# A vision tokenizer kernel on one core: the product steps of a group placed one step later in TensorE's list

## The chip, the core and the metric

The kernel runs on one core of a Trainium2 chip. A core has a matrix engine (TensorE, PE in the profile, with its weight loads listed apart as PEld), a vector engine (VectorE, DVE), a scalar engine (ScalarE, ACT), GpSimd (POOL), SyncE (SP), which here only starts transfers, and DMA queues. Each engine works through its own list of instructions in order; a list waits for another only at a semaphore. The metric is the time of one execution on the device in microseconds (us). Of three runs of the kernel before, the median is 921.68 us (920.68 to 923.33).

## The reference, cut to what matters

```python
def tokens(x, gamma, beta, W, b):            # x: (64, 2, 104, 104)
    lu, ru, ld, rd = _shifts(x)              # the image moved by 4 pixels in four directions
    concat = jnp.concatenate((x, lu, ru, ld, rd), axis=1)
    mean = jnp.mean(concat, axis=(1, 2, 3), keepdims=True)
    var = jnp.var(concat, axis=(1, 2, 3), keepdims=True)
    normed = (concat - mean) * jax.lax.rsqrt(var + EPS)
    normed = normed * gamma[None] + beta[None]
    y = conv(normed, W, window_strides=(8, 8))   # 13 x 13 patches, 128 outputs each
    return (y + b).reshape(B, E, -1).transpose(0, 2, 1)
h = tokens(x, ...)
h = jnp.concatenate([cls_tok, h], axis=1)        # 170 tokens for each image
h = h + attention(_layernorm(h), ...)            # gated linear attention
h = h + experts(_layernorm(h), ...)              # 8 experts, 2 for each token
```

The change concerns the first stage, `tokens`, and the layer-norm statistics of its result.

## The kernel before

The program has three stages one after the other: tokens (to about 197 us), attention with routing (to about 540 us), experts and the final sums (to the end). Only the first is touched.

**Tiling.** The 64 images are worked on in 8 groups of 8, a group as 4 pairs of images; a pair has 340 tokens, which are 3 tiles of 128. For group g, in this order: SyncE loads the images (`load_group`), ScalarE sums and squares (`stats_squares`), VectorE copies and sums the edges (`stats_sums`, L1022 on), TensorE adds over the rows of an image (`stats`, L701 on), VectorE makes mean and variance (`stats_small`), ScalarE the reciprocal deviation (`rstd`), VectorE the shift (`shifts`), ScalarE the normalised image (`normalise`) and VectorE its edges (`normalise_edges`). Then TensorE turns patches into columns in 8 **fills** of PSUM (`transpose_fill`, L669 on, matmul line L680; fills 0 to 3 have 4, 3, 3, 3 transposes, fills 4 to 7 have 4, 4, 3, 3), and VectorE multiplies each fill by gamma into the arena (`scale_fill`, line L1066). When all eight are scaled, TensorE makes the group's tokens in 6 **product blocks** (`y_tiles`, line L697), each 10 matmuls, that is two tiles of five matmuls (the trace counts each of these matmuls twice). A pair is complete halfway in blocks 1 and 4 and at the end of blocks 2 and 5. VectorE adds the bias to a complete pair and stores it in h (`tokens_out`, L1088) and later takes its layer-norm statistics (`ln1_stats`, lines L1094 and L1098). After the last pair ScalarE and VectorE turn the statistics into factors (L1639, L1640), and the attention stage begins.

**What sets the order.** The lists are written by hand. In both engines `group(g, ...)` walks through steps k = 0 to 7: TensorE transposes fill k of group g and does a product block of group g - 1; VectorE scales fill k of group g and does the tokens and statistics of groups g - 1 and g - 2 and the image statistics of group g + 1. `group` is called for g = 0 to 8; for g = 8 there is nothing left to transpose (`tr=False`), for g = 0 there are no products (`y=False`), and for g = 7 and 8 no image statistics (`stat=False`). Below, F0 to F7 are the transposes of the fills and Y0 to Y5 the product blocks in TensorE's list.

**The waits that matter here:**

- Y0 of a group waits until VectorE has scaled all its fills (`tr_free`, first line of `y_tiles`).
- The fill of step k may be transposed when the fill four before it has been scaled (`tr_free`): four PSUM banks are used in turn.
- The four small matmuls of `stats(g + 1)`, at k = 3 after the fill, wait for `dsum_done`, which VectorE's `stats_sums(g + 1)` gives, and for `asum_done`, which ScalarE gives after squaring the edges that `stats_sums` has copied (L1478).
- `tokens_out` waits for its pair (`y_full`); the products of a pair wait for a free one of three banks (`h_added`).

Of the kernel before, what the change touches and what calls it, by code (L numbers as in the profile page):

```python
# [28 lines left out]
GPAIRS = GROUP // 2  # L29
PT = 2 * TOK  # L30
PTILES = -(-PT // 128)
# [80 lines left out]
def need(eng, sem, value):  # L112

    if not isinstance(value, int) or value > 0:
        eng.wait_ge(sem, value)
# [44 lines left out]
def build(nc, a, out_rows):  # L160
# [6 lines left out]
    with ExitStack() as ctx:  # L167
# [454 lines left out]
        def _(pe):  # L622
# [39 lines left out]
            def beta_turn():  # L662
                pe.wait_ge(S["bt_copied"], 2)
                for t in range(PTILES):
                    ins = pe.transpose(ps[5][:, 128 * t:128 * t + 128], bt_t[:, 128 * t:128 * t + 128], ident)
                ins.then_inc(S["bt_turned"], 1)
# [4 lines left out]
            def transpose_fill(g, par, k):  # L671
                if k == 0:
                    pe.wait_ge(S["xmn_done"], g + 1)
                if k == 4:
                    pe.wait_ge(S["xhn_done"], g + 1)
                    pe.wait_ge(S["xen_done"], g + 1)

                need(pe, S["tr_free"], 8 * g + k - 3)
                for n, (src, rows) in enumerate(fills[par][k]):
                    ins = pe.transpose(ps[k % 4][:, rows * n:rows * n + rows],  # L680
                                       src.rearrange("r a b -> r (a b)"), ident[0:rows, 0:rows])
                ins.then_inc(S["tr_full"], 1)

            def y_tiles(g, par, k):

                if k == 0:
                    pe.wait_ge(S["tr_free"], 8 * g + 8)
                for j in range(2 * k, 2 * k + 2):
                    pair, t = j // PTILES, j % PTILES
                    q = GPAIRS * g + pair  # L690
                    if t == 0:
                        need(pe, S["h_added"], q - len(TOKEN_BANKS) + 1)
                        if q == 1:
                            pe.wait_ge(S["bt_ready"], 1)
                    at = PT * pair + 128 * t
                    for s in range(NSHIFT):
                        ins = pe.matmul(ps[TOKEN_BANKS[q % len(TOKEN_BANKS)]][:, 128 * t:128 * t + 128],  # L697
                                        gx_all[par][:, s, at:at + 128], wt[:, s, :], start=s == 0, stop=s == NSHIFT - 1)
                    if t == PTILES - 1:
                        ins.then_inc(S["y_full"], 1)  # L700

            def stats(g):
                pe.wait_ge(S["dsum_done"], g + 1)
                pe.wait_ge(S["asum_done"], g + 1)
                need(pe, S["var_done"], g)
                x0 = cols["stat_all"][0]
                x1 = cols["stat_edge"][0]
                for k in range(2):
                    o = ps[6][0:HROWS, 2 * k:2 * k + 2]
                    pe.matmul(o, cst[0:HROWS, x0 + k * HROWS:x0 + (k + 1) * HROWS], st[0:HROWS, 0:2], start=True, stop=False)  # L710
                    ins = pe.matmul(o, cst[0:HROWS, x1 + k * HROWS:x1 + (k + 1) * HROWS], st[0:HROWS, 2:4],
                                    start=False, stop=True)
                ins.then_inc(S["stat_ps"], 1)

            def group(g, par, tr=True, y=True, stat=True):
                for k in range(8):
                    if tr:
                        transpose_fill(g, par, k)
                    if (g, k) == (1, 0):
                        beta_turn()  # L720
                    if k == 3 and stat:
                        stats(g + 1)
                    if 1 <= k <= GPAIRS * PTILES // 2 and y:
                        y_tiles(g - 1, 1 - par, k - 1)

            patch_transposes(0, "gam_flat", "gam_ps")
            stats(0)
# [242 lines left out]
        def _(dve):  # L970
# [23 lines left out]
            def beta_out():  # L994
                dve.wait_ge(S["cleared"], CLEAR_BET)
                dve.wait_ge(S["bet_ps"], 1)
                patches_out(1, "bet_ready")
# [24 lines left out]
            def stats_sums(g, par, u):  # L1022
                dve.wait_ge(x_loaded[par], 16 * GROUP_DMAS * (u + 1))

                need(dve, S["xen_done"], g)
                need(dve, S["asum_done"], g)
                need(dve, S["stat_ps"], g)
                x3 = xh[par][0:HROWS, :].rearrange("r (cp w) -> r cp w", w=SIDE)
                ch.link(dve.tensor_copy(xe[0:HROWS, 0, :, HALF:PATCH], x3[:, :, 0:HALF]))
                dve.tensor_copy(xe[0:HROWS, 1, :, 0:HALF], x3[:, :, SIDE - HALF:SIDE]).then_inc(S["edge_done"], 1)  # L1030
                dve.wait_ge(S["edge_done"], g + 1)
                dve.tensor_reduce(st[0:HROWS, 2:3], xe[0:HROWS].rearrange("r a b c -> r (a b c)"), AX_X, ALU.add)\
                   .then_inc(S["dsum_done"], 1)

            def stats_small(g):
                dve.wait_ge(S["stat_ps"], g + 1)
                m = st[0:HROWS, 4:8].rearrange("r (k a) -> r k a", k=2)
                ch.link(dve.tensor_scalar(st[0:HROWS, 4:8], ps[6][0:HROWS, 0:4], 1.0 / N_CONCAT, None, ALU.mult))
                ch.link(dve.tensor_tensor(st[0:HROWS, 8:10], m[:, :, 0], m[:, :, 0], ALU.mult))
                dve.tensor_tensor(st[0:HROWS, 10:12], m[:, :, 1], st[0:HROWS, 8:10], ALU.subtract).then_inc(S["var_done"], 1)  # L1040
# [42 lines left out]
            def tokens_out(g, k):  # L1083

                dve.wait_ge(S["y_full"], GPAIRS * g + k + 1)
                src = ps[TOKEN_BANKS[(GPAIRS * g + k) % len(TOKEN_BANKS)]][:, 0:PCOLS].rearrange("p (t n) -> p t n", t=PTILES)
                hp = h[:, bass.ds(GPAIRS * g + k, 1), :, :].rearrange("p o t n -> p (o t) n")
                dve.tensor_tensor(hp, src, bt[:, :, :], ALU.add).then_inc(S["h_added"], 1)  # L1088

            def ln1_stats(g, k):  # L1090
                dve.wait_ge(S["h_added"], GPAIRS * g + k + 1)
                need(dve, S["ln1_stats"], GPAIRS * g + k - 1)
                for t in range(PTILES):
                    ch.step(dve.bn_stats(bns1[:, k % 2, t], h[:, bass.ds(GPAIRS * g + k, 1), t, :].rearrange("p o n -> p (o n)")))  # L1094
                ch.settle()
                for t in range(PTILES):
                    tile = bass.ds(PTILES * GPAIRS * g + PTILES * k + t, 1)
                    ins = dve.bn_aggr(mv1[:, tile, :].rearrange("p o m -> p (o m)"), bns1[:, k % 2, t])  # L1098
                    if t < PTILES - 1:
                        ch.step(ins)  # L1100
                ins.then_inc(S["ln1_stats"], 1)

            def group(g, par, base, u, tr=True, y=True, stat=True):
                ch.start(base)
                for k in range(8):
                    if k == 1 and stat:
                        stats_sums(g + 1, 1 - par, u)
                    if k == 4 and stat:
                        stats_small(g + 1)
                    if k in (3, 4, 6, 7) and y:  # L1110
                        tokens_out(g - 1, (3, 4, 6, 7).index(k))
                    if k == 5 and stat:
                        shifts(g + 1)
                    if tr:
                        scale_fill(g, par, k)
                    if (g, k) == (0, 2):
                        beta_out()
                    if (g, k) == (0, 4):
                        weights_out()
                    if (g, k) == (0, 7):  # L1120
                        beta_products_out()
                    if (g, k) == (1, 0):
                        beta_tokens_out()
                    if k in (0, 1) and g >= 2:
                        ln1_stats(g - 2, k + 2)
                    if k in (5, 7) and y:
                        ln1_stats(g - 1, (5, 7).index(k))
                    if k == 6 and stat:
                        normalise_edges(g + 1, 1 - par)
                if not tr:  # L1130
                    for k in range(2, GPAIRS):
                        ln1_stats(g - 1, k)
                return ch.n
# [16 lines left out]
            for g in range(1, NGROUP - 1):  # L1150
                dbase += group(g, g % 2, dbase, (g + 1) // 2)
# [563 lines left out]
```

## Time and profile before

| | |
|---|---|
| median of 3 runs | 921.68 us (920.68 to 923.33) |
| profiled execution | 921.47 us, span from first to last instruction 919.7 us |
| busy: PE, PEld | 801.1 us (87%), 684.4 us (74%) |
| busy: DVE, ACT, POOL | 743.3 us (81%), 571.0 us (62%), 504.0 us (55%) |
| mean granted TensorE clock | 0.943 of full speed |
| chain that ended last, shares of the whole | PE 47%, DVE 28%, issue 10% |
| the product blocks, L697 | 960 matmuls in the trace, 123.9 us busy, idle before them 12.0 us, ended by DVE's L1066 |
| scaling of fills, L1066 | 160 instructions, 71.8 us busy, idle before them 12.7 us, ended by PE's L680 |

The profile is of one execution, so sums are made against its 921.47 us. "Idle before" is time in which the engine did nothing, and the releaser is what it had been waiting for. A granted clock of 1.00 is 2.4 GHz, 0.50 is 1.2 GHz. Matmuls overlap each other, so the time that the trace gives for a row of them reaches a little beyond the start of the next row; the distance between two starts is the better measure.

### The profile page before, as it was taken

The page shows a single profiled execution, that of the slowest core. Times are in us where ns is not written, and L with a number is a line of the kernel's source. Part 1 is how long each engine was busy: PE and PEld are TensorE (multiplying, and loading weights), DVE is VectorE, ACT ScalarE, POOL GpSimd, SP SyncE. Part 2 cuts the span into 40 slices and gives each one's busy share as a digit, 9 for nine tenths or more (in the row PEclk, how much of TensorE's full clock was granted, in tenths as well). Part 3 has the DMA queues.
Part 4 walks back from the last instruction along what each step waited for, and adds up shares of the span by engine and source line. Part 5 has one row for each costly group of instructions (what it writes and reads, how often), then busy time and mean ns, then how long its engine had stood idle before and what let it go on. Part 6 is the DMA issues. An engine that isn't in the chain of part 4 may idle for free.

```text
span 919.7 us, 27974 instructions
## 1 busy us (share of the span) xinstructions
PE 801.1 (87%) x7821; PEld 684.4 (74%) x7822; DVE 743.3 (81%) x3194; ACT 571.0 (62%) x1536; POOL 504.0 (55%) x660
## 2 busy tenths in 40 slices
PE   1799999888999999999999638999999999999910
PEld 1699999875677777777777526999999999999910
DVE  2768777833789999989999752999999999999987
ACT  2633344015889999999999523666676666676610
POOL 3000000000078888888788782778877777877850
PEclk9999999998999999999999558999999999999965
DMA  8544330034011212122121226422222222222489
GB/s 181 124 80 82 61 62 1 1 115 144 23 55 54 60 57 62 54 60 60 51 63 55 63 86 206 164 80 76 79 73 76 74 74 73 80 74 76 125 299 376
DMA packets 68637, 84.19 MB, mean 92 GB/s; under 512 B 12118, under 2 KB 52745, under 8 KB 68157
## 3 DMA queue, kind: packets, MB, share of 16 engines
q1 hardware_dynamic: 52727, 53.27, 21.4%
q0 software_dynamic: 12256, 22.50, 7.9%
q10 hardware_dynamic: 3555, 7.23, 2.3%
q8 instruction: 49, 0.80, 0.4%
q14 instruction: 50, 0.39, 0.2%
HBM read 48.15 MB, written 35.71 MB: 91 GB/s over the span
## 4 chain that ended last, share of the span: by engine, by line
PE 47%; DVE 28%; issue 10%; ACT 4%; DMA 3%; SPq 2%; DVEq 2%; ACTq 1%; POOL 1%; POOLq 0%
PE ps L697 9%; DVE arena L1400 7%; PE ps L797 5%; DVE arena L1066 4%; PE ps L772 4%; DVE arena L1421 3%; PE ps L783 3%; PE ps L846 3%; PE ps L832 3%; PE ps L851 3%; PE ps L778 2%; DVE arena L1383 2%; PE ps L865 2%; PE ps L956 2%; PE ps L761 2%
## 5 line engine op out<-in xcount | busy, mean ns | idle before, releaser
L578 POOL DMA_INDIRECT x_slots<-arena x192 | 191.9, 1000 | 58.1 <-POOL arena L576 45.7
L607 POOL DMA_INDIRECT y_tokens<-arena x184 | 187.4, 1018 | 46.1 <-issue 45.2
L956 PE MATMUL ps<-arena 128*128 x1472 | 180.5, 276 | 0.2 <-ACT arena L1663 0.2
L956 PEld LDWEIGHTS ps<-arena 128*128 128x128 f32 x1472 | 171.6, 192 | 1.6 <-issue 0.3
L1663 ACT ACTIVATE arena<-ps,b_t 128x256 f32<-128x256 f32 x368 | 144.6, 475 | 29.1 <-PE ps L947 19.8
L697 PE MATMUL ps<-wt,arena 128*128 128x128 f32 x960 | 123.9, 289 | 12.0 <-DVE arena L1066 12.0
L697 PEld LDWEIGHTS ps<-wt,arena 128*128 128x128 f32 x960 | 118.5, 203 | 13.4 <-DVE arena L1066 13.4
L583 POOL MEMSET arena<- 128x258 f32 x1 | 0.3, 319 | 193.6 <-DVE arena L1317 193.6
L945 PE MATMUL ps<-arena 128*128 128x256 f16 x368 | 101.3, 275 | 5.1 <-DVE arena L1369 5.1
L946 PE MATMUL ps<-arena 128*128 128x256 f16 x368 | 101.2, 275 | 0.0
L947 PE MATMUL ps<-arena 128*128 128x256 f16 x368 | 101.1, 275 | 0.0
L1400 DVE TENSOR_SCALAR arena<-arena 128x128 f32<-128x128 f32 x184 | 90.2, 533 | 0.1
L599 POOL TENSOR_TENSOR arena<-arena 128x256 f32<-128x256 f32 x92 | 64.8, 704 | 36.1 <-DVE arena L1376 26.4
L1066 DVE TENSOR_TENSOR arena<-ps,arena 128x312 f32<-128x312 f32 (+2 forms) x160 | 71.8, 501 | 12.7 <-PE ps L680 12.7
L576 POOL MEMSET arena<- 1x256 f32 x168 | 50.8, 302 | 49.7 <-ACT arena L1545 49.0
L1527 ACT ACTIVATE arena<-ps 128x340 f32<-128x340 f32 (+3 forms) x160 | 67.6, 442 | 11.5 <-PE ps L761 3.6
L1670 ACT ACTIVATE arena<-arena,cst 128x2 f32<-128x2 f32 x92 | 27.4, 298 | 76.0 <-DVE arena L1390 75.5
L1199 DVE TENSOR_TENSOR arena<-ps,cst 85x340 f32<-85x340 f32 x128 | 58.8, 499 | 11.4 <-PE ps L797 11.2
L1369 DVE TENSOR_TENSOR arena<-ps,arena 128x256 f16<-128x256 f32 x92 | 38.1, 414 | 33.4 <-ACT arena L1655 30.0
L1421 DVE SCALAR_TENSOR_TENSOR arena<-arena 128x128 f32<-128x128 f32 x184 | 56.9, 351 | 0.0
L797 PE MATMUL ps<-arena 32*85 32x170 f32 x512 | 52.7, 322 | 0.7 <-DVE arena L1199 0.7
L1655 ACT ACTIVATE arena<-ps 128x256 f16<-128x256 f32 x92 | 36.9, 401 | 22.1 <-PE ps L930 22.1
(216 smaller groups left out, 1785.2 us busy)
## 6 DMA issues: line engine op xcount, KB each, us to landing
arena<-x_slots SPq DMA_DIRECT2D x92, 130.0 KB
h<-h_rows SPq DMA_DIRECT2D x1, 5440.0 KB
arena<-y_tokens SPq DMA_DIRECT2D x17, 320.0 KB
out<-h ACTq DMA_DIRECT2D x17, 320.0 KB, 3.5
arena<-x_in SPq DMA_DIRECT2D x64, 84.5 KB
arena<-x_in SPq DMA_DIRECT2D x56, 78.0 KB
h_rows<-h SPq DMA_DIRECT2D x32, 128.0 KB
arena<-y_tokens SPq DMA_DIRECT2D x1, 3200.0 KB, 14.8
```

Of the source, the lines that this page charges most:

```text
L578: pool.indirect_dma_start(xs_dram, bass.IndirectOffsetOnAxis(ap=slot_i[n][0:rows, t, k:k + 1], axis=0), row[n][0:rows, k, t, :], None).the ...
L607: pool.indirect_dma_start(y_dram, bass.IndirectOffsetOnAxis(ap=y_id[n % YBUF][:, k:k + 1], axis=0), y_sl[n % YBUF][:, k, :], None, bounds_ ...
L697: ins = pe.matmul(ps[TOKEN_BANKS[q % len(TOKEN_BANKS)]][:, 128 * t:128 * t + 128], gx_all[par][:, s, at:at + 128], wt[:, s, :], start=s == ...
L797: ins = pe.matmul(o, kd[par][r, chunk(c)], qd[par][r, :, chunk(c)], start=True, stop=True, tile_position=(at, 0))
L945: pe.matmul(o, hi, x_hi[m], start=True, stop=False)
L946: pe.matmul(o, hi, x_lo[m], start=False, stop=False)
L947: pe.matmul(o, lo, x_hi[m], start=False, stop=True).then_inc(S["h_ps"], 1)
L956: ins = pe.matmul(ps[6 + m][:, 128 * k:128 * k + 128], hid[m][:, c, 128 * k:128 * k + 128], w2_sb[:, bass.ds(e, 1), c, :].rearrange("p o n ...
L1066: return dve.tensor_tensor(dst, src, gm, ALU.mult)
L1400: ins = dve.tensor_scalar(nrm[:, k, :], res[n % 2][:, k, :], mv3[:, k, 0:1], rg3[:, k:k + 1], ALU.subtract, ALU.mult)
L1421: ins = dve.scalar_tensor_tensor(y_sl[n % YBUF][:, k, :], be, g[:, k:k + 1], scl[:, k, :], ALU.mult, ALU.add)
L1663: act.activation(hid[m][:, c, :], ps[2 + 2 * m + c // 2][:, SLOT * (c % 2):SLOT * (c % 2) + SLOT], ACT.Relu, bias=b1_t[:, bass.ds(e * FC + ...
```

## The change

TensorE's product blocks stand at steps 2 to 7 instead of 1 to 6. VectorE's `tokens_out` follows: the four pairs of a group were taken at steps 3, 4, 6 and 7, and are now taken at 4, 5 and 7 and at step 0 of the next group. `ln1_stats` of the first two pairs moves from steps 5 and 7 to 6 and 7, that of the last two from steps 0 and 1 of the next group to 0 and 2. In the call for g = 8 the last `tokens_out` now stands behind the loop over k. No instruction is added or removed.

```diff
@@ TensorE, group(g, par, ...)
-                    if 1 <= k <= GPAIRS * PTILES // 2 and y:
-                        y_tiles(g - 1, 1 - par, k - 1)
+                    if 2 <= k and y:
+                        y_tiles(g - 1, 1 - par, k - 2)
@@ VectorE, group(g, par, ...)
-                    if k in (3, 4, 6, 7) and y:
-                        tokens_out(g - 1, (3, 4, 6, 7).index(k))
+                    if k == 0 and g >= 2:
+                        tokens_out(g - 2, GPAIRS - 1)
+                    if k in (4, 5, 7) and y:
+                        tokens_out(g - 1, (4, 5, 7).index(k))
...
-                    if k in (0, 1) and g >= 2:
-                        ln1_stats(g - 2, k + 2)
-                    if k in (5, 7) and y:
-                        ln1_stats(g - 1, (5, 7).index(k))
+                    if k in (0, 2) and g >= 2:
+                        ln1_stats(g - 2, 2 + k // 2)
+                    if k in (6, 7) and y:
+                        ln1_stats(g - 1, k - 6)
...
                 if not tr:
+                    tokens_out(g - 1, GPAIRS - 1)
                     for k in range(2, GPAIRS):
                         ln1_stats(g - 1, k)
```

TensorE's list before, from Y5 in the call for g = 2 to F2 in the call for g = 3 (L680: transposes of a fill, ps0 to ps3 its bank; L697: products; L710, further on: the first of the statistics matmuls):

```order
L697 MATMUL ps5<-wt,arena 128x128 x10
L680 MATMUL ps3<-cst,arena 128x112 [waits tr_free]
L680 MATMUL ps3<-cst,arena 128x112 x2
L680 MATMUL ps0<-cst,arena 128x104 [waits tr_free,xmn_done]
L680 MATMUL ps0<-cst,arena 128x104 x3
L680 MATMUL ps1<-cst,arena 128x104 [waits tr_free]
L680 MATMUL ps1<-cst,arena 128x104 x2
L697 MATMUL ps7<-wt,arena 128x128 [waits h_added,tr_free]
L697 MATMUL ps7<-wt,arena 128x128 x9
L680 MATMUL ps2<-cst,arena 128x104 [waits tr_free]
```

The same place now, from F7 (bank ps3) to the statistics matmuls in the call for g = 3:

```order
L680 MATMUL ps3<-cst,arena 128x112 [waits tr_free]
L680 MATMUL ps3<-cst,arena 128x112 x2
L697 MATMUL ps5<-wt,arena 128x128 x10
L680 MATMUL ps0<-cst,arena 128x104 [waits tr_free,xmn_done]
...
L680 MATMUL ps1<-cst,arena 128x104 [waits tr_free]
...
L680 MATMUL ps2<-cst,arena 128x104 [waits tr_free]
L680 MATMUL ps2<-cst,arena 128x104 x2
L697 MATMUL ps7<-wt,arena 128x128 [waits h_added,tr_free]
L697 MATMUL ps7<-wt,arena 128x128 x9
L680 MATMUL ps3<-cst,arena 128x104 [waits tr_free]
L680 MATMUL ps3<-cst,arena 128x104 x2
L710 MATMUL ps6<-st,cst 112x2 [waits var_done,asum_done,dsum_done]
```

Y5, the first row of the piece before, now stands behind F7; Y0, the block that waits for the scaling of F7, stands behind F0, F1 and F2 of the next group, and F3 and the statistics matmuls follow it directly, without the Y1 that stood between.

VectorE's list before, from the end of the scaling of F7 (g = 1) to the first two instructions of `stats_sums` (L1094 and L1098: layer-norm statistics; L1088: `tokens_out`; L1029 and L1030: the copies of `stats_sums`):

```order
L1066 TENSOR_TENSOR arena<-ps3,arena 128x8x13x3
L1094 BN_STATS bns1<-h 128x6 [waits h_added]
L1094 BN_STATS bns1<-h 128x6 x2
L1098 BN_AGGR mv1<-bns1 128x2 [waits dch]
L1098 BN_AGGR mv1<-bns1 128x2 x2
L1066 TENSOR_TENSOR arena<-ps0,arena 128x8x13x4 [waits y_full,tr_full]
L1094 BN_STATS bns1<-h 128x6 [waits ln1_stats,h_added]
L1094 BN_STATS bns1<-h 128x6 x2
L1098 BN_AGGR mv1<-bns1 128x2 [waits dch]
L1098 BN_AGGR mv1<-bns1 128x2 x2
L1029 COPY arena<-arena 112x16x4 [waits asum_done,stat_ps,xen_done,xl1]
L1030 COPY arena<-arena 112x16x4 [waits dch]
```

The same place now:

```order
L1066 TENSOR_TENSOR arena<-ps3,arena 128x8x13x3
L1094 BN_STATS bns1<-h 128x6 [waits h_added]
L1094 BN_STATS bns1<-h 128x6 x2
L1098 BN_AGGR mv1<-bns1 128x2 [waits dch]
L1098 BN_AGGR mv1<-bns1 128x2 x2
L1088 TENSOR_TENSOR h<-ps4,bt 128x384 [waits y_full]
L1066 TENSOR_TENSOR arena<-ps0,arena 128x8x13x4 [waits y_full,tr_full]
L1094 BN_STATS bns1<-h 128x6 [waits ln1_stats,h_added]
L1094 BN_STATS bns1<-h 128x6 x2
L1098 BN_AGGR mv1<-bns1 128x2 [waits dch]
L1098 BN_AGGR mv1<-bns1 128x2 x2
L1029 COPY arena<-arena 112x16x4 [waits asum_done,stat_ps,xen_done,xl1]
```

One `tokens_out` has come in ahead of `stats_sums`. A little earlier in the same list, between the scaling of F6 and `normalise_edges`, one `ln1_stats` has come in as well; it stood ahead of the scaling of F6 before.

The end of VectorE's part in the stage, in the call for g = 8, before (ps4 and ps5 are the banks of the last two pairs; two more pieces like L1094 to L1098 follow):

```order
L1088 TENSOR_TENSOR h<-ps4,bt 128x384 [waits y_full]
L1088 TENSOR_TENSOR h<-ps5,bt 128x384 [waits y_full]
L1094 BN_STATS bns1<-h 128x6 [waits ln1_stats,h_added]
L1094 BN_STATS bns1<-h 128x6 x2
L1098 BN_AGGR mv1<-bns1 128x2 [waits dch]
L1098 BN_AGGR mv1<-bns1 128x2 x2
```

And now, with two such pieces behind the last `tokens_out` as well, this being the first row of the first:

```order
L1088 TENSOR_TENSOR h<-ps4,bt 128x384 [waits y_full]
L1094 BN_STATS bns1<-h 128x6 [waits ln1_stats,h_added]
L1094 BN_STATS bns1<-h 128x6 x2
L1098 BN_AGGR mv1<-bns1 128x2 [waits dch]
L1098 BN_AGGR mv1<-bns1 128x2 x2
L1088 TENSOR_TENSOR h<-ps5,bt 128x384 [waits y_full]
L1094 BN_STATS bns1<-h 128x6 [waits ln1_stats,h_added]
```

The statistics of the second pair have moved from behind the last `tokens_out` to ahead of it: three pieces stood behind it, and two do now.

## Rows read from the trace of the kernel before

**Rows 1.** Windows: length, busy us (instructions) by engine, granted clock, DMA share, GB/s.

```profile
84.76:103.49 18.73, 17.05 (x155) 16.85 (x156) 15.55 (x57) 7.60 (x10) 0.00 (x0) 1.00 0.40 78
103.49:123.83 20.34, 18.68 (x156) 18.48 (x156) 15.72 (x57) 7.60 (x10) 0.00 (x0) 0.92 0.33 64
182.14:197.43 15.29, 15.29 (x121) 15.29 (x122) 5.17 (x27) 0.00 (x0) 0.00 (x0) 0.89 0.00 1
```

**Rows 2.** Timeline of TensorE over one group: start, length, instructions, idle before and releaser.

```profile
84.76 2.50 PE L697 MATMUL ps<-wt,arena 128*128 128x128 f32 x20 [1.67 <-DVE arena L1066]
87.10 0.43 PE L680 MATMUL ps<-cst,arena 104*128 104x104 f32 x3
87.37 2.42 PE L697 MATMUL ps<-wt,arena 128*128 128x128 f32 x20
89.62 0.43 PE L680 MATMUL ps<-cst,arena 104*128 104x104 f32 x3
89.89 0.28 PE L710 MATMUL ps<-st,cst 112*112 112x2 f32 x2
...
98.19 0.45 PE L680 MATMUL ps<-cst,arena 112*128 112x112 f32 x3
...
100.73 1.08 PE L680 MATMUL ps<-cst,arena 112*128 112x112 f32 x10
103.49 4.13 PE L697 MATMUL ps<-wt,arena 128*128 128x128 f32 x20 [1.68 <-DVE arena L1066]
```

**Rows 3.** Timeline of TensorE in later groups and at the stage's end.

```profile
109.98 0.43 PE L680 MATMUL ps<-cst,arena 104*128 104x104 f32 x3
...
123.83 4.01 PE L697 MATMUL ps<-wt,arena 128*128 128x128 f32 x20 [1.66 <-DVE arena L1066]
...
164.54 2.50 PE L697 MATMUL ps<-wt,arena 128*128 128x128 f32 x20 [1.66 <-DVE arena L1066]
...
179.72 0.45 PE L680 MATMUL ps<-cst,arena 112*128 112x112 f32 x3
182.14 15.29 PE L697 MATMUL ps<-wt,arena 128*128 128x128 f32 x120 [1.97 <-DVE arena L1066]
```

**Rows 4.** Timeline of VectorE over the same group as Rows 2, and one later row.

```profile
87.23 0.19 DVE L1029 COPY arena<-arena 112x64 f32<-112x64 f32 x1
...
98.15 0.67 DVE L1094 BATCH_NORM_STATS2 bns<-h 128x6 f32<-128x128 f32 x3
...
99.21 0.53 DVE L1088 TENSOR_TENSOR h<-ps,bt 128x384 f32<-128x384 f32 x1
99.65 1.66 DVE L1066 TENSOR_TENSOR arena<-ps,arena 128x312 f32<-128x312 f32 x4
...
102.00 1.44 DVE L1066 TENSOR_TENSOR arena<-ps,arena 128x208 f32<-128x208 f32 x4
103.34 0.68 DVE L1094 BATCH_NORM_STATS2 bns<-h 128x6 f32<-128x128 f32 x3
...
105.97 0.19 DVE L1029 COPY arena<-arena 112x64 f32<-112x64 f32 x1
...
110.45 0.48 DVE L1066 TENSOR_TENSOR arena<-ps,arena 128x312 f32<-128x312 f32 x1 [0.83 <-PE ps L680]
```

**Rows 5.** Timeline of ScalarE: the squares of the edges.

```profile
87.75 0.42 ACT L1478 ACTIVATE arena<-arena 112x256 bf16<-112x256 f32 x1 [4.28 <-DVE arena L1030]
88.07 0.19 ACT L1478 ACTIVATION_READ_ACCUMULATOR arena<-arena 112x1 f32 x1
```

**Rows 6.** Timeline of VectorE at the stage's end: two of the last statistics.

```profile
199.32 0.65 DVE L1094 BATCH_NORM_STATS2 bns<-h 128x6 f32<-128x128 f32 x3
...
200.35 0.65 DVE L1094 BATCH_NORM_STATS2 bns<-h 128x6 f32<-128x128 f32 x3
```

**Rows 7.** Windows, columns as in Rows 1: the start of the attention stage.

```profile
204.00:212.00 8.00, 5.13 (x30) 3.24 (x30) 1.45 (x4) 4.15 (x10) 0.00 (x0) 0.87 1.11 305
212.00:220.00 8.00, 8.00 (x55) 4.79 (x53) 2.27 (x5) 2.41 (x7) 0.00 (x0) 0.71 0.66 232
```

## The prediction

> **What bounds the kernel now.** I read the profile's page first: TensorE is busy 87% of the span and stands first in the chain of waits, VectorE second. That is a mean over three stages, and only the first, to about 197 us, is touched. So I read next the busy time by windows over this stage. An undisturbed group lasts 18.73 us, TensorE is busy for 17.05 of them and VectorE for 15.55 [rows 1]: both are nearly full, and what one can hide from the other is small. The chain of waits hands over once a group: product blocks on TensorE, then from F5 on VectorE's work, then Y0. The timeline of TensorE shows where: one wait in a group, 1.67 us idle ahead of Y0, for VectorE's L1066, the scaling of F7 [rows 2]. Y0 needs F7 scaled, and before it TensorE has nothing but F0 and F1 to do, while VectorE has a statistics step, two tokens steps, the edges and two scalings. This wait occurs seven times, for groups 2 to 7 and, with 1.97 us, ahead of the last 120 matmuls [rows 2, 3].
>
> The windows show a second loss at the same places. The granted clock is 1.00 in the group from 84.76 us but 0.92 in the one from 103.49, which lasts 20.34 us [rows 1]; its Y0 takes 4.13 us instead of 2.50 [rows 2]. So it goes three times, the second at 123.83, and once more in the last 120 matmuls, at clock 0.89 [rows 1, 3]. Each time the clock falls from 2.4 to 1.2 GHz directly behind the end of this wait; in the groups where it doesn't, the windows show 1.00 throughout.
>
> **The wait ahead of Y0: removed.** The listed idle time starts at the modelled end of the last transpose; by starts the loss is larger. F7, F0 and F1 are ten transposes, 1.08 us from 100.73, of which 0.43 - (87.37 - 87.10) = 0.16 is overlap, so Y0 could have started at 101.65. It started at 103.49: 1.84 us. A Y0 after a wait also takes 87.10 - 84.76 = 2.34 us to the next row, a Y1 2.25 [rows 2]: 0.09 more. That is 1.93 for each of six groups, 11.6 us. For the last, F7 starts at 179.72, takes 98.19 to 100.73 less a block, 0.29, and Y0 starts at 182.14 [rows 2, 3]: 2.13 us. Together 13.7 us.
>
> Is anything left of it? Now Y5 stands behind F7. I count from the start of F6. VectorE starts scaling 0.47 us after the transposes (109.98 to 110.45) [rows 3, 4], and reaches the end of the scaling of F7 after its work from 99.65 to 103.44 (102.00 + 1.44), 3.79, plus the statistics step that now stands in between, 99.21 - 98.15 = 1.06 [rows 4]: 5.32. TensorE does F6, Y4, F7, Y5 in 2 x 2.54 = 5.08 and F0, F1, F2 in 0.92 - 0.29 + 0.27 = 0.90, so it comes to Y0 at 5.98. Cleared by 0.66. For the last 120 matmuls there are no F0 to F2 behind Y5, but VectorE has no edges to normalise either, so its 5.32 is an upper bound against 5.08: at most 0.24 us remain, and I take 0.
>
> **A new wait at the statistics.** The four matmuls of `stats` stand at k = 3 as before, but one block less precedes them in the group, while VectorE's `stats_sums`, on which they wait, has moved back behind one more statistics step and one more tokens step. Again from F6: TensorE reaches them after 5.98 + 2.25 (Y0) + 0.27 (F3; 89.62 to 89.89) = 8.50 us [rows 2]. VectorE starts `stats_sums` at 0.47 + (105.97 - 99.65 = 6.32) + 1.06 + (99.65 - 99.21 = 0.44) = 8.29 [rows 4]. From its start at 87.23 to the end of ScalarE's sum at 88.07 + 0.19 = 88.26 [rows 4, 5] is 1.03, and 0.05 for the hand-over (103.44 to 103.49 [rows 2, 4]): 9.37. So TensorE waits 0.87 us and restarts at a loss of 0.09: 0.96, in groups 2 to 6, which have `stats`: 4.8 us given back. Before, this wait did not exist: 88.31 was long past at 89.89. Behind the waiting matmuls are Y1 and F4, and VectorE waits for them; that shifts the rest of the group by the same amount, and F6 starts as far ahead of VectorE as before, so that the wait stays at 0.87 from group to group instead of growing. The trace of before doesn't contain this wait. Its bounds are 0, if VectorE is a microsecond quicker than its row spacing says, and the 1.93 of the wait removed. I take the 0.96 from the rows nearest to it.
>
> **The other moves.** The first pair's tokens step stands at k = 4 and its pair is complete halfway in Y1, just ahead of F4: no later than its neighbours need it. The second pair's step waits for the end of Y2, and the scaling of F4 now stands ahead of it and fills the time. The transposes wait for the fill four before, which is scaled more than a block earlier. ScalarE needs 7.6 us in a group [rows 1] and its normalised image is used a block and more after it is ready. No wait of this stage after 45 us names a transfer. The loads start, as before, when the group that had their buffer has been normalised. All this at nothing; it is hidden by TensorE's 17 us a group.
>
> **The clock.** The three groups cost 20.34 - 18.73 = 1.61 us more each, 4.8 us. The last block takes 15.29 against 6 x 2.25 + 0.16 + 0.09 = 13.75: 1.54 us [rows 1, 2, 3]. Together 6.4 us. Waits of 1.68, 1.66 and 1.97 us were followed by the lower level, of 1.67 and 1.66 (84.76 and 164.54) not [rows 2, 3]. So a wait of this length stands just at the edge of it, and one of 0.87 us on the safe side. I take all 6.4 us as won; the other end is below nothing, if each of the five new waits is followed by it: 6.4 - 8.0 = -1.6 us.
>
> On this the Trainium skill (TensorE: Matmul & The Clock Gate, "Why this matters for your kernels") says otherwise: no gaps of more than about 3 us, since only an idle window throttles. The trace does not agree, it fell after 1.68 us. By that rule the low stretches aren't due to these waits and would stay; that is the second rival below. The same page, Part 4, says that transposes don't count as busy like other matmuls. If so, the stretch without products was 1.08 + 1.68 = 2.76 us here and becomes at most F3, wait and `stats`, 0.27 + 0.87 + 0.73: still shorter, so the sum stays.
>
> **The tail.** After the last product VectorE did one tokens step and three statistics steps. Now that of the second pair stands ahead of the last tokens step and is done while TensorE still works; one step less is 200.35 - 199.32 = 1.03 us [rows 6], on the path to the attention stage.
>
> **Sum.** 13.7 - 4.8 + 6.4 + 1.0 = 16.3 us, against the profiled 921.47 us: 905.2. The median before is 0.2 higher; I say 905.3 us.
>
> **Rivals.**
> 1. No new wait: VectorE gets to `stats_sums` in time, because its steps run closer where TensorE's blocks don't hold it up. For it: VectorE's idle 0.83 us at F3 [rows 4] shows that it has room elsewhere. Against: between F6 and `stats_sums` the rows show no idle time. 905.3 - 4.8 = 900.5 us.
> 2. The low clock stays, by one stretch for most of the waits as now: 905.3 + 6.4 = 911.7 us, or 913.3 with five. For it: the edge is thin, and the skill's rule. Against: 0.87 is half of any wait that was followed by it.
> 3. Given back later: the attention stage starts at a different moment of the clock's. Its start is at 0.87 and 0.71 now [rows 7], (0.13 + 0.29) x 8 / 0.5 = 6.7 us at the lower level, at most 3.4 us of loss, which may vanish or double: 902 to 908.7 us.
> 4. Slower than before: the new wait, at `stats` in the middle of the product blocks, drops TensorE's clock for long. The moves without the clock save 13.7 - 4.8 + 1.0 = 9.9 us, and low stretches of 1.6 us already cost 6.4. It would take 16.3 us, ten stretches, two for each new wait, to come to nothing; at three for each, 24 us, the time is 905.3 + 24 = 929 us. Against: the trace has never more than one in a row in this stage.
> 5. The order doesn't do what it says: excluded by the lists, which show F7 ahead of Y5.
>
> **How the numbers follow.** The forecast with rival 3 inside it has 0.70, its own range 902 to 909. No new wait 0.10, low clock stays 0.16, slower 0.03, and 0.01 for a return to no change by a mixture. For 8 in 10 I take 900.2 to 912.0: it holds the first two rivals' central values. A difference of 0.3%, 2.8 us, is about what a measurement of this kernel can tell from none; faster by more than that has 0.95, within it 0.02, slower 0.03.
>
> **What would show it.** In the timeline of TensorE: no idle ahead of Y0 and Y5 directly behind F7; 0.9 us idle ahead of L710 in five groups, released by ScalarE's L1478; groups of about 17.8 us; granted clock 1.00 from 50 us to the end of the products; these ending near 182 us; two statistics steps behind the last tokens step. The prediction is wrong if L710 does not wait, if it waits over 1.5 us, or if windows of the stage show 0.92 again.

## The result

The changed kernel takes 904.52 us (median of 6 runs, 901.72 to 909.9), the kernel before in the same comparison 921.18 us (6 runs, 917.96 to 923.33): ratio 0.9839, 95% interval 0.9813 to 0.9865, so 16.7 us faster by the medians; 905.3 had been forecast. The ratio and its interval are worked out from the single runs: they make 14.8 us (12.4 to 17.2), where the two medians alone would give 0.9819. In a second comparison (e1 below) it was 903.74 against 917.74 us, 0.9859 (0.9817 to 0.9902). Executions fall into a faster and a slower state; ratios in this document compare runs in the faster one, and medians are over all runs. The profiled execution took 907.38 us, its span is 905.6 us.

The page's fifth part of the changed kernel, products and fills (line, engine, operation | busy us, mean ns | idle before and its releaser):

```profile
L697 PE MATMUL ps<-wt,arena 128*128 128x128 f32 x960 | 117.3, 279 | 0.0
L1066 DVE TENSOR_TENSOR arena<-ps,arena 128x312 f32<-128x312 f32 (+2 forms) x160 | 71.5, 503 | 12.3 <-PE ps L680 12.3
```

The 12.0 us of idle time ahead of the products are gone, and they are 6.6 us less busy, since behind the first block of the stage none runs at the lower clock. Windows over one group and over the last 140 products of the changed kernel, columns as in [rows 1]:

```profile
107.12:124.93 17.81, 17.01 (x156) 16.84 (x156) 15.57 (x57) 7.60 (x10) 0.00 (x0) 1.00 0.39 78
169.92:185.65 15.73, 15.73 (x142) 15.72 (x141) 8.82 (x42) 0.00 (x0) 0.00 (x0) 1.00 0.01 2
```

A group takes 17.81 us where it took 18.73 or 20.34 [rows 1], with the same busy times; the clock is 1.00 in both windows. The first product block, at 49.05 us, takes 4.51 us, as long as one at the lower clock, although the windows there show 1.00; the kernel before has the same at 45.59 us, with 4.26. TensorE's timeline in the changed kernel, over the turn of a group:

```profile
97.96 2.41 PE L697 MATMUL ps<-wt,arena 128*128 128x128 f32 x20
100.20 0.45 PE L680 MATMUL ps<-cst,arena 112*128 112x112 f32 x3
100.49 2.41 PE L697 MATMUL ps<-wt,arena 128*128 128x128 f32 x20
102.74 1.06 PE L680 MATMUL ps<-cst,arena 104*128 104x104 f32 x10
103.63 2.42 PE L697 MATMUL ps<-wt,arena 128*128 128x128 f32 x20
105.89 0.43 PE L680 MATMUL ps<-cst,arena 104*128 104x104 f32 x3
107.12 0.33 PE L710 MATMUL ps<-st,cst 112*112 112x2 f32 x2 [0.80 <-DVE st L1032]
107.90 2.48 PE L697 MATMUL ps<-wt,arena 128*128 128x128 f32 x20
...
124.93 0.33 PE L710 MATMUL ps<-st,cst 112*112 112x2 f32 x2 [0.80 <-DVE st L1032]
...
169.63 0.45 PE L680 MATMUL ps<-cst,arena 112*128 112x112 f32 x3
169.92 15.89 PE L697 MATMUL ps<-wt,arena 128*128 128x128 f32 x140
185.65 4.68 PE L748 MATMUL ps<-cst 128*128 128x384 f32 x14
190.87 0.55 PE L761 MATMUL ps<-cst,arena 128*128 128x128 f32 x3 [0.54 <-ACT arena L1525]
```

Y5 (100.49) stands directly behind F7, Y0 (103.63) directly behind F0, F1 and F2, in place of [rows 2]; L710 waits, five times in all (0.79 to 0.81 us idle). At the end the last products follow F7 without a gap, in place of 2.13 us in [rows 3]. VectorE and ScalarE over the same turn:

```profile
98.16 1.65 DVE L1066 TENSOR_TENSOR arena<-ps,arena 128x312 f32<-128x312 f32 x4 [0.30 <-PE ps L680]
99.73 0.67 DVE L1094 BATCH_NORM_STATS2 bns<-h 128x6 f32<-128x128 f32 x3
...
101.55 1.46 DVE L1066 TENSOR_TENSOR arena<-ps,arena 128x208 f32<-128x208 f32 x4
102.91 0.67 DVE L1094 BATCH_NORM_STATS2 bns<-h 128x6 f32<-128x128 f32 x3
...
105.99 0.20 DVE L1029 COPY arena<-arena 112x64 f32<-112x64 f32 x1
...
106.45 0.42 DVE L1032 TENSOR_REDUCE st<-arena 112x1 f32<-112x256 f32 x1
106.51 0.42 ACT L1481 ACTIVATE arena<-arena 112x256 bf16<-112x256 f32 x1 [3.99 <-DVE arena L1030]
...
106.83 0.19 ACT L1481 ACTIVATION_READ_ACCUMULATOR arena<-arena 112x1 f32 x1
```

The scaling of F7 is done at 103.01, 0.62 us before Y0 could start. From F6's scaling to L1029 it is 7.83 us; 6.32 + 1.06 + 0.44 = 7.82 had been added up from [rows 4]. The view names VectorE's L1032 as what L710 waited for; that ended at 106.87, ScalarE's sum (L1478 before, L1481 here) at 107.02, and L710 starts at 107.12. For a wait on several semaphores the ends have to be compared by hand. That ScalarE's was the last is read from the ends; no run changes ScalarE's part alone.

The spans differ by 14.1 us, less than the medians. By pieces of the two timelines: from F0 of group 1 to the start of the L748 matmuls 155.13 us before, 140.56 now, 14.6 less; from there to the first transposes of the attention stage 6.57 and 5.22, 1.35 less; from there to the end 715.9 and 714.7, 1.1 less; but F0 of group 1 itself starts at 45.09 instead of 42.14, 2.95 us later. The later start begins with ScalarE's wait for the images of group 1. ScalarE's timeline, before:

```profile
28.85 1.59 ACT L1471 ACTIVATE arena<-arena 112x1664 bf16<-112x1664 f32 x1 [1.85 <-DMA arena<-x_in]
```

and in the changed kernel:

```profile
31.79 1.59 ACT L1474 ACTIVATE arena<-arena 112x1664 bf16<-112x1664 f32 x1 [3.58 <-DMA arena<-x_in]
```

### The profile page after: what moved, and what is told of

Same layout as the page of the kernel before. It is cut to its first block, busy times and chain, and to the rows that moved or that the text cites. A ratio compares the mean times of both kernels' runs of the same rounds, so it can differ in the third digit from the quotient of the medians.

```text
span 905.6 us, 27974 instructions
## 1 busy us (share of the span) xinstructions
PE 793.7 (88%) x7821; PEld 677.8 (75%) x7822; DVE 743.0 (82%) x3194; ACT 570.5 (63%) x1536; POOL 502.5 (55%) x660
## 4 chain that ended last, share of the span: by engine, by line
PE 53%; DVE 20%; issue 9%; DMA 5%; ACT 4%; SPq 2%; POOL 2%; DVEq 2%; ACTq 1%; POOLq 0%
PE ps L697 9%; DVE arena L1403 5%; PE ps L956 5%; PE ps L797 5%; PE ps L772 4%; PE ps L783 3%; PE ps L846 3%; PE ps L832 3%; PE ps L851 3%; PE ps L778 2%; DVE arena L1066 2%; PE ps L865 2%; DVE arena L1424 2%; PE ps L761 2%; DMA arena<-y_tokens 2%
## 5 line engine op out<-in xcount | busy, mean ns | idle before, releaser
L697 PE MATMUL ps<-wt,arena 128*128 128x128 f32 x960 | 117.3, 279 | 0.0
L697 PEld LDWEIGHTS ps<-wt,arena 128*128 128x128 f32 x960 | 112.6, 195 | 0.0
```

## The experiments

e1 to e4 ran on one chip, e5 to e12 on another. There every kernel took much longer: before was at 986.5 us beside e5 to e8 and at 1018.2 us beside e9 to e12, with runs from 973 to 1010 and from 1003 to 1039 us. The time was lost behind the tokens stage: in e8's profile the attention stage lasts 404 us at a mean clock of 0.88, in e1's 352 us at 0.94. In the tokens stage the row spacing of equal lists agrees to a few hundredths wherever the clock is the same. So for e5 to e12 the stage's rows decide, and totals are given but carry little. The changed kernel itself did not run beside e5 to e12.

| | median us | ratio to before | 95% interval |
|---|---|---|---|
| e1, the changed kernel again | 903.74 | 0.9859 | 0.9817 to 0.9902 |
| e2, `stats_sums` first | 901.82 | 0.9831 | 0.9791 to 0.9871 |
| e3, before with its wait filled | 915.55 | 0.9983 | 0.9957 to 1.0009 |
| e4, TensorE's half | 918.27 | 1.0001 | 0.9976 to 1.0026 |
| e5, a longer wait | 990.54 | 1.0061 | 0.9999 to 1.0124 |
| e6, the tail as before | 980.96 | 0.9959 | 0.9911 to 1.0008 |
| e7, VectorE's half | 992.90 | 1.0051 | 0.9984 to 1.0117 |
| e8, as e2 | 970.36 | 0.9839 | 0.9740 to 0.9937 |
| e9, as e2 | 1004.09 | 0.9905 | 0.9852 to 0.9958 |
| e10, as e5 | 1016.82 | 1.0049 | 1.0002 to 1.0095 |
| e11, as e7 | 1026.40 | 1.0120 | 1.0036 to 1.0203 |
| e12, as e6 | 1009.05 | 0.9957 | 0.9906 to 1.0007 |

**e1, the changed kernel again, without an edit.**

> The changed kernel once more, beside the others on the same chip: 904.5 us within 2.5, so 0.981 to 0.984 of before. Both theories say the same. In the trace: group spacing of TensorE 17.8 us, 0.8 us idle ahead of the first statistics matmul in five groups. If the 3 us by which the loads of the second group came later in the profiled run belong to the change, they are there again; if they are a matter of the single run, the first transposes of group 1 start near 42 us as before.

The median came out as expected, the ratio a little above (0.9859). The five waits of L710 and the group spacing of 17.81 are there again. F0 of group 1 starts at 44.99 us; but it starts at 45.12 in e3 as well, whose lists up to there are those of before, and at 43.66 in e4. In all twelve experiments it lies between 43.66 and 48.92. So the later start belongs to the run, not to the change; the profiled run of before, with 42.14 us, was an early one.

**e2, e8, e9: one statistics step less ahead of `stats_sums`.**

```diff
-                    if k in (0, 2) and g >= 2:
-                        ln1_stats(g - 2, 2 + k // 2)
+                    if k in (1, 2) and g >= 2:
+                        ln1_stats(g - 2, 1 + k)
```

> The changed kernel with one statistics step (ln1_stats of the third pair) moved from step 0 to step 1, behind stats_sums and the scaling of fill 1. Theory: VectorE's list decides the new wait; 1.06 us less ahead of stats_sums against a wait of 0.96 by starts: the wait is gone in all five groups, groups of 16.8 us, 4.8 us less: 899.7 us. Rival (the wait is ScalarE's, or it only moves to a later place, since VectorE is nearly full): 904.5 us, with idle time of TensorE ahead of another row.

All three engines in e2 at the place of the wait:

```profile
69.81 0.19 DVE L1029 COPY arena<-arena 112x64 f32<-112x64 f32 x1
...
70.64 0.19 ACT L1481 ACTIVATION_READ_ACCUMULATOR arena<-arena 112x1 f32 x1
70.81 0.43 PE L680 MATMUL ps<-cst,arena 104*128 104x104 f32 x3
...
71.08 0.27 PE L710 MATMUL ps<-st,cst 112*112 112x2 f32 x2
```

ScalarE's sum is done at 70.83, L710 starts 0.27 us behind F3, as in a list without a wait, and no other wait of TensorE appears in the stage. From F0 of group 1 to L748 it is 134.82 us, in e1 139.11; the first Y0, part of it as slow as at the lower clock, took 3.94 against 3.17. That makes 4.29 + 0.77 = 5.06 us for five waits, 1.01 each. Shown: VectorE's order is what makes the wait, and it is gone. Of the 5 us only 1.9 show in the medians (901.82 where 899.7 had been expected, and 903.74 in e1).

> The kernel with stats_sums ahead of the statistics step once more. In its profile the stage was 4.8 us shorter than in the changed kernel, but its median only 1.9 us. Theory (chance of the runs: arrival of the first loads, one low stretch at the start of the expert stage): median 898.5 to 901. Rival (the rest really gives 3 us back, whenever the stage ends earlier): 901.8 us again, and the stages behind it longer by 3 us in the profile again.

> The kernel of e2 and e8 again, since the times of e8's call were disturbed behind the tokens stage. Theory: 4.8 us less than the changed kernel in the stage reach the end: ratio to before 0.980 to 0.982 where the changed kernel had 0.984 to 0.986. Rival (given back behind the stage): 0.983 again.

In e8 and e9 the stage is again without a wait (F0 of group 1 to the attention stage 139.60 and 139.84 us; 140.04 in e2, 144.33 in e1). The totals don't tell theory from rival: the interval of e8 (0.9740 to 0.9937) holds both, that of e9 (0.9852 to 0.9958) neither. What the record does show of the missing 3 us in e2 is a lower clock. In its profile the stages behind are 4.8 us longer than in e1's; summed over windows of 1 us, TensorE's clock is at its lower level there for 92.6 us against 86.9, which at half speed is at most 2.9 us. That run was the longest of its six, but the others lean the same way: the mean granted clock of the six is 0.9488, that of e1's six 0.9513, an estimated 0.0025 x 903 = 2.3 us. Whether the earlier end of the stage brings this about is open.

**e3: the wait of Y0 filled with work, in the kernel before.**

```diff
+                    if k == 1 and g >= 2:
+                        for _ in range(2):
+                            pe.matmul(ps[6][:, 128:512], ident, cst[:, 0:PCOLS], start=True, stop=True)
                     if 1 <= k <= GPAIRS * PTILES // 2 and y:
                         y_tiles(g - 1, 1 - par, k - 1)
```

> The kernel before with two matmuls without use (1.3 us of 384 columns) ahead of each wait of Y0, in the time in which TensorE had nothing to do; the wait itself stays. Theory: the low clock comes from the idle time of this wait, so the four low stretches (6.4 us) vanish while the order and the start of Y0 stay as before: 914.8 us, clock 1.00 from 50 to 197 us. Rival (the low stretches are not due to the wait): 921.2 us with 0.92 in three groups. If the filling delays Y0: over 921.

TensorE's timeline in e3; L725 is the filling:

```profile
84.25 1.08 PE L680 MATMUL ps<-cst,arena 112*128 112x112 f32 x10
85.17 1.48 PE L725 MATMUL ps<-cst 128*128 128x384 f32 x4
87.01 2.50 PE L697 MATMUL ps<-wt,arena 128*128 128x128 f32 x20 [0.37 <-DVE arena L1069]
...
179.53 13.66 PE L697 MATMUL ps<-wt,arena 128*128 128x128 f32 x120 [0.68 <-DVE arena L1069]
```

Y0 starts every 18.72 us, in all groups (68.29, 87.01, 105.75, 124.47 and on), and the last 120 products take 13.66 instead of 15.29 us [rows 3]. From 54 us on no low clock is left in the stage, with the order as before and Y0 still waiting, 0.35 to 0.68 us. That alone would prove little, as e7 below has waits of 1.75 us and no low stretch behind six of them. What shows the tie is the whole of the profiles: none of 38 waits of up to 1.11 us was followed by the lower clock, 21 of 32 waits of 1.65 us and more were, and a longer wait in e5 and e10 brings low stretches into the changed kernel. Their size in the median is far below the 6.4 us: 2.2 us less than before, or 1.6 by the ratio, with an interval of -0.8 to 3.9 us. The runs of before beside e3 reach from 911.41 to 924.88 us; the profiled one of 921.47 us, from which the 6.4 us were read, is slower than all but three of these 23.

**e4: TensorE's half alone** (the first hunk of the diff, VectorE's list as before).

> TensorE's half of the change alone: its blocks at steps 2 to 7, VectorE's list as before. Theory: VectorE's half is needed, because its tokens steps at 3, 4, 6 and 7 now wait for blocks that come later and hold up the scalings behind them; the scaling of F7 ends about 7.3 us behind the start of F6 instead of 5.3, Y0 waits 1.3 us and the statistics matmuls 1.0 us: groups of 19.3 us, 924 us, up to 932 with low clock. Rival (TensorE's order alone gives the gain): 905 us.

TensorE's timeline in e4, its two waits:

```profile
66.99 2.50 PE L697 MATMUL ps<-wt,arena 128*128 128x128 f32 x20 [1.11 <-DVE arena L1066]
...
70.59 0.33 PE L710 MATMUL ps<-st,cst 112*112 112x2 f32 x2 [0.83 <-DVE st L1032]
...
86.18 2.50 PE L697 MATMUL ps<-wt,arena 128*128 128x128 f32 x20 [1.11 <-DVE arena L1066]
```

Two waits a group and 19.19 us from Y0 to Y0 (19.3 expected), the clock at 1.00 in these groups, and no low stretch behind the last wait of 2.00 us either. The longer groups and the absence of low stretches come out at before's time in this comparison, 918.27 against 917.74 us, not at the 924 us expected. The rival is out: TensorE's order alone gives nothing.

**e7, e11: VectorE's half alone** (the other hunks; TensorE's blocks at steps 1 to 6).

> VectorE's half of the change alone, TensorE's list as before. Theory: the two halves are worth little apart. From F5 to the end of the scaling of F7 VectorE's list is one tokens step shorter (0.45 us), so Y0 waits 1.4 us instead of 1.9 by starts, seven times 0.45 us, and the tail's 1.0 us: 4 us less than before, 913.5 us against 917.7; groups of 18.3 us. Rival (VectorE's half carries the gain): 904 to 906 us.

VectorE's scalings of F4 to F7, and TensorE's Y0, in e7:

```profile
76.81 1.87 DVE L1066 TENSOR_TENSOR arena<-ps,arena 128x416 f32<-128x416 f32 x4 [1.70 <-PE ps L680]
...
79.44 2.08 DVE L1066 TENSOR_TENSOR arena<-ps,arena 128x416 f32<-128x416 f32 x4 [0.23 <-PE ps L680]
...
81.98 1.65 DVE L1066 TENSOR_TENSOR arena<-ps,arena 128x312 f32<-128x312 f32 x4 [0.45 <-PE ps L680]
...
85.37 1.43 DVE L1066 TENSOR_TENSOR arena<-ps,arena 128x208 f32<-128x208 f32 x4
86.86 2.50 PE L697 MATMUL ps<-wt,arena 128*128 128x128 f32 x20 [1.75 <-DVE arena L1066]
```

The expectation was wrong. The groups are 18.80 us long, not 18.3, and Y0 waits 1.75 us. VectorE is ahead of TensorE at F6 (0.45 us idle, none before [rows 4]), since the statistics and tokens steps that filled this time before now stand elsewhere, the statistics step behind the scaling of F6. From the start of F6 to the end of F7's scaling it is 5.31 us (81.49 to 86.80), where it was 5.25 (98.19 to 103.44). A step taken out of a list is no gain where the list then waits. What is left of this half is the tail: 0.54 us ahead of the attention stage, as in the changed kernel.

> The kernel of e7 again. In its profile the wait of Y0 did not shrink (1.75 us), because the scaling of F6, which now directly follows that of F5, waits for TensorE's F6. Theory now: only the tail's 1.0 to 1.3 us remain: ratio to before 0.997 to 1.000. Rival (the first expectation): 0.995.

Neither theory nor rival: the ratio is 1.0120 (1.0036 to 1.0203), a loss. In the profiled run of e11, the longest of its seven with 1064.94 us, the stage's rows show a part of it. TensorE's timeline:

```profile
72.29 4.13 PE L697 MATMUL ps<-wt,arena 128*128 128x128 f32 x20 [1.73 <-DVE arena L1066]
92.72 4.13 PE L697 MATMUL ps<-wt,arena 128*128 128x128 f32 x20 [1.76 <-DVE arena L1066]
...
193.75 13.66 PE L697 MATMUL ps<-wt,arena 128*128 128x128 f32 x120 [2.05 <-DVE arena L1066]
```

The kernel is that of e7 and the six waits are about as long, 1.73 to 1.76 us, but each of the six is followed by the lower clock, and the groups last 20.43 instead of 18.80 us. Only behind the last wait, of 2.05 us, it is the other way round: a low stretch in e7 (15.29 us), none here. That is six stretches of 1.6 us against one. For the ratio an estimate can be made from the clocks of the runs that it compares: on average 0.9045 against before's 0.9162, 0.0117 x 1010 = 11.8 us, about the 1.2% lost. In which stage those runs lost it is not known.

**e5, e10: a longer wait at `stats`.**

```diff
-                    if k in (0, 2) and g >= 2:
-                        ln1_stats(g - 2, 2 + k // 2)
+                    if k == 0 and g >= 2:
+                        ln1_stats(g - 2, 2)
+                        ln1_stats(g - 2, 3)
```

> The changed kernel with both late statistics steps (third and fourth pair) at step 0, so ahead of stats_sums. Theory: the new wait grows by one statistics step, 1.06 us, to 1.86 us idle by the profile, in five groups: 5.3 us more than the changed kernel; and as idle times of 1.66 to 1.97 us sometimes brought the lower clock before, it comes back behind some of them, 1.6 us each: 909 to 917 us, likeliest 912, and a wider spread of the runs. Rival (the clock doesn't depend on these waits): 909 us and clock 1.00 throughout the stage.

TensorE in e5, two of five groups:

```profile
92.29 0.33 PE L710 MATMUL ps<-st,cst 112*112 112x2 f32 x2 [1.83 <-DVE st L1032]
93.07 4.11 PE L697 MATMUL ps<-wt,arena 128*128 128x128 f32 x20
...
112.76 0.33 PE L710 MATMUL ps<-st,cst 112*112 112x2 f32 x2 [1.83 <-DVE st L1032]
113.54 4.10 PE L697 MATMUL ps<-wt,arena 128*128 128x128 f32 x20
```

The wait grew from 0.80 to 1.83 us, by one statistics step, and behind each of the five the block runs at the lower clock, 4.1 instead of 2.5 us. Groups are 20.47 us long: 17.81 + 1.03 + 1.63. The rival is out for this run.

> The kernel of e5 again. Its profile showed 1.83 us idle in five groups and the lower clock behind all five. Theory: 5 x (1.06 + 1.6) = 13.3 us more than the changed kernel: ratio to before 0.999 to 1.001, so nearly all of the gain gone. Rival (the low clock of the profiled run was chance and few runs have it): 5 us more, 0.990.

Again five of five, with blocks of 4.05 to 4.09 us. The gain over before is gone: the ratios are 1.0061 and 1.0049, the second with an interval from 1.0002 just above the 0.999 to 1.001 expected and far from the rival's 0.990. In the same two comparisons the kernel of e2 stands at 0.9839 and 0.9905.

**e6, e12: the last group's statistics step back behind the last tokens step.**

```diff
-                    if k in (6, 7) and y:
+                    if k in (6, 7) and y and (tr or k == 6):
                         ln1_stats(g - 1, k - 6)
...
                     tokens_out(g - 1, GPAIRS - 1)
-                    for k in range(2, GPAIRS):
+                    for k in range(1, GPAIRS):
```

> The changed kernel with the last group's statistics of the second pair back behind the last tokens step, as before. Theory: one statistics step more on the path to the attention stage: 1.03 to 1.35 us more, first transposes of the attention stage 6.6 us instead of 5.2 us behind the start of the matmuls of L748: 905 us. Rival (the path there is TensorE's own seven matmuls): no change, 903.7 us, and still 5.2 us.

TensorE's timeline in e6, ahead of the attention stage:

```profile
184.06 4.68 PE L748 MATMUL ps<-cst 128*128 128x384 f32 x14
190.63 0.55 PE L761 MATMUL ps<-cst,arena 128*128 128x128 f32 x3 [1.90 <-ACT arena L1525]
```

6.57 us between the two rows, against 5.22 in the changed kernel: the tail's move is worth 1.35 us, on the path. The rival is out.

> The kernel of e6 again. In its profile the first transposes of the attention stage waited 1.90 us instead of 0.54. Theory: 1.3 us more than the changed kernel, less than the runs of one call can tell. Rival (the shorter idle time there also spares low clock at the start of the attention stage): 3 us more or above, ratio to before 0.988 or above.

1.90 us again. The ratio, 0.9957, lies above the 0.988 of the rival, but the changed kernel did not run beside it, and its own ratio under these conditions isn't known. Open.

## Why the prediction was right

- **The wait ahead of Y0.** Forecast: seven waits gone, 13.7 us, VectorE 0.66 us ahead at Y0 and a tie at the last block. Measured: no wait, 0.62 us, and at the last block the scaling of F7 ends at 172.09 (170.65 + 1.44 in VectorE's timeline) where Y5 ends at about 172.17 (its start at 169.92 and the 2.25 us of a block). No bound had to be used.
- **The new wait at `stats`.** Forecast 0.87 us by starts and 0.09 of restart; measured 107.12 - (105.89 + 0.27) = 0.96 and 0.05 (L710 to Y1 0.78 us instead of 0.73), five times. e2 takes it away, e5 lengthens it by a step. The releaser promised, ScalarE's sum over the edges, is the last by the ends of the rows; the view itself names VectorE's L1032.
- **Groups.** 17.81 us against "about 17.8". In the stage from F0 of group 1 to L748 the forecast was 13.7 - 4.8 + 6.4 = 15.3, the profiles show 14.6: the waits cost 0.25 more, and the first Y0, F2 and F3, in the slow start of the stage, took 0.6 us longer than in the profiled run of before, while the last low stretch was 0.1 us dearer than reckoned. The products ended at 185.65 us, not near 182, mostly because the run began the group work 2.95 us later.
- **The clock.** The direction held: no low stretch is left behind these waits. Its size did not, and it is the term that was mis-sized. 6.4 us are right for the profiled run of before, with its four stretches; over many runs e3 finds 2.2 by the medians and at most 3.9 by the ratio. The prediction took one profiled run for the rule. The granted clocks of all runs of the second comparison agree with the smaller figure: on average 0.9481 for before, 0.9502 for e3, 0.9513 for the changed kernel. As a microsecond at the lower level costs half of one where TensorE is busy, the difference of 0.0032 makes an estimated 2.9 us. With 13.7 - 5.05 for the waits and 1.35 for the tail that is 12.9 us, which is also what the ratio of 0.9859 makes of 917.74. The forecast of 16.3 lies within both intervals (12.4 to 17.2 and 9.0 to 16.8 us), but that it meets the 16.7 us of the first pair of medians so closely is in part luck: before ran at 921.2 us there and at 917.7 in the second. How much the clock gave in the first comparison is not on record.
- **The rule on idle gaps.** What the Trainium skill says of them (TensorE: Matmul & The Clock Gate, "Why this matters for your kernels", no idle gaps over about 3 us) does not agree with these traces: ten waits of 1.8 us brought ten low stretches, six of 1.75 us in e11 six, and with the wait filled in e3 none followed. Of what Part 4 of that page says on transposes no run tells anything, as a row of ten of them at 102.74 stands between full-clock blocks and nothing longer was tried.
- **The tail.** Forecast 1.03, measured 1.35: the step that left the path was the first behind the last tokens step, and in e6 that one takes 186.11 - 184.73 = 1.38 us (by its L1094 rows), the others 1.04. The row of [rows 6] was that of the cheaper ones. Two statistics steps stand behind the last tokens step, as forecast.
- **Rivals.** No new wait: out, by the trace. Low clock stays, and slower by low clock: not in this kernel; e5 shows what they would have been. Given back later: in the first 20 us of the attention stage the clock is 0.83 before and after, 6.8 us at the lower level, so nothing there.

The kernel of e2 is the fastest measured: 901.82 us, 0.9831 (0.9791 to 0.9871) of before, 1.9 us below the changed kernel in the same comparison.

## What to carry to other kernels

When one engine waits once a period for another, lay out both lists from a common row and add up the starts; that gives the wait removed and the next one, here to a tenth of a microsecond, and it needs both halves of the change (e4 and e7 gain nothing). Before a step is moved ahead or back, ask whether its engine was idle there: a step that filled a wait costs nothing where it stood. Where low clock appears only in some groups, take its price from many runs and not from the one that was profiled: the same kernel with the same waits had no low stretch behind six of them in one profile (e7) and six in another (e11).

## What the runs showed of the hardware

How the granted clock followed idle times of TensorE in this stage, in all profiles, from 60 us on:

| idle us | kernel | low stretch behind it |
|---|---|---|
| 0.35 to 0.68 | e3 | 0 of 7 |
| 0.77 to 0.84 | changed, e1, e4, e6, e12 | 0 of 25 |
| 1.10 to 1.11 | e4 | 0 of 6 |
| 1.65 to 1.69 | before | 3 of 6 |
| 1.73 to 1.77 | e7 | 0 of 6 |
| 1.73 to 1.76 | e11, the kernel of e7 | 6 of 6 |
| 1.81 to 1.84 | e5, e10 | 10 of 10 |
| 1.97 to 2.05 | before, e4, e7, e11 | 2 of 4 |

A low stretch cost 1.6 us each time. Its occurrence isn't a matter of the idle time alone, since the same waits of 1.75 us brought none in e7 and six in e11. Low stretches come in series: where one followed such a wait, and the group was 20.34 to 20.47 us long, the next such wait at 1.66 to 1.84 us brought one too in 15 of 16 cases (2 of 3 in before, 5 of 5 in e11, 4 of 4 in e5 and in e10); in e7, with groups of 18.80 us and none at the start, none came for six waits. What starts a series no run shows. Idle times up to 1.11 us brought none in 38.
